# An eight-expert feed-forward layer with its tokens sorted by expert

## The reference, cut to what matters

```python
gate_scores = softmax(x @ Wg + bg)                      # 2048 tokens, 8 experts
top1_mask   = one_hot(argmax(gate_scores), 8)           # one expert a token
top1_weight = sum(gate_scores * top1_mask)
h = silu(einsum('btd,edh->bteh', x, W1) + b1)           # 256 -> 1024, each expert
o = einsum('bteh,ehd->bted', h, W2) + b2                # 1024 -> 256
x = layernorm(x + sum(o * top1_mask) * top1_weight)
```

## Time and profile before

| what | value |
|---|---|
| device time, median of 3 runs (lowest, highest) | 6390.07 us (6388.35, 6396.14) |
| device time of the profiled execution | 6391.87 us |
| its span from first to last instruction | 6390.1 us |
| mean granted TensorE clock over the span (1 is 2.4 GHz) | 0.816 |
| `L0_ffn`: first transfer of the stage, first one behind it | 2192.07 us, 3164.54 us |

### The profile page before, as it was taken

The page is one execution under the profiler, slowest core; times in us unless marked ns, Lnnn a source line. Parts: engine busy times, 40 slices in busy tenths (PEclk is TensorE's granted clock), DMA queues, the critical chain, the costliest instruction groups (busy, mean ns, idle before and its releaser), DMA issues. The chain is left out here.

```text
span 6390.1 us, 128995 instructions
## 1 busy us (share of the span) xinstructions
PE 4716.8 (74%) x51675; PEld 3223.8 (50%) x51683; DVE 3581.3 (56%) x9434; ACT 1403.9 (22%) x2503; POOL 1043.7 (16%) x1087
## 2 busy tenths in 40 slices
PE   2766767667677499999887774576685577787797
PEld 1555555555555356666555552343463345565454
DVE  7889898898894300000255455588244445444445
ACT  1222222222222121121122223111133322231111
POOL 1223232232232200000122220000010012221000
PEclk7888888888889699999988886555686687888899
DMA  1110111111100100000000000000000000000000
GB/s 49 29 28 21 29 29 26 28 25 29 29 20 22 42 14 13 26 13 13 8 0 0 31 7 12 3 0 0 36 0 5 5 4 0 26 3 6 10 17 25
DMA packets 51863, 109.59 MB, mean 17 GB/s; under 512 B 5520, under 2 KB 43792, under 8 KB 49296
## 3 DMA queue, kind: packets, MB, share of 16 engines
q1 hardware_dynamic: 51344, 102.21, 5.6%
HBM read 98.78 MB, written 3.41 MB: 16 GB/s over the span
## 5 line engine op out<-in xcount | busy, mean ns | idle before, releaser
L1603 PE MATMUL psum<-arena 128*128 128x512 f32 x1600 | 706.6, 595 | 58.4 <-DVE Y L1667 35.8
L1684 DVE SCALAR_TENSOR_TENSOR Y<-psum,arena,Y 128x256 f32<-128x256 f32 x416 | 172.5, 477 | 847.9 <-PE psum L1615 847.9
L1615 PE MATMUL psum<-arena 128*128 128x256 f32 x2624 | 583.0, 380 | 4.1 <-DVE arena L1708 4.1
L754 POOL TENSOR_TENSOR weights<-weights,arena 128x64 f32<-128x64 f32 x512 | 395.7, 794 | 1042.4 <-DVE arena L1272 1042.3
L1615 PEld LDWEIGHTS psum<-arena 128*128 128x128 f32 x2624 | 499.3, 190 | 111.7 <-issue 43.5
L144 POOL TENSOR_TENSOR arena<-arena,eps 128x4 f32<-128x4 f32 (+2 forms) x76 | 16.3, 214 | 3214.1 <-DVE arena L139 3214.1
L1603 PEld LDWEIGHTS psum<-arena 128*128 128x128 f32 x1600 | 304.4, 191 | 409.1 <-issue 341.4
L1322 DVE TENSOR_TENSOR arena<-arena 128x120 f32<-128x120 f32 (+27 forms) x1888 | 398.1, 252 | 4.3 <-DVE arena L1315 2.7
L831 PE MATMUL psum<-arena 128*32 128x1 bf16 x639 | 114.2, 179 | 385.7 <-DVE arena L1284 301.1
L1315 DVE TENSOR_TENSOR arena<-arena 128x120 f32<-128x120 f32 (+27 forms) x1888 | 390.3, 246 | 6.4 <-DVE arena L1322 2.9
L422 PE MATMUL psum<-ident,arena 128*128 128x128 f32 x1280 | 217.5, 325 | 210.4 <-ACT arena L493 210.4
(11 more groups left out here) (419 smaller groups left out, 8347.5 us busy)
## 6 DMA issues: line engine op xcount, KB each, us to landing
weights<-L_decay_rows SPq DMA_DIRECT2D x256, 160.0 KB, 3.5
arena<-in_experts_L_ffn SPq DMA_DIRECT2D x8, 2052.0 KB, 7.5
arena<-in_ctxT SPq DMA_DIRECT2D x16, 512.0 KB, 3.2
arena<-in_experts_L_ffn SPq DMA_DIRECT2D x18, 384.0 KB, 3.0
weights<-in_w_L_ffn SPq DMA_DIRECT2D x1, 3072.0 KB, 9.9
weights<-in_w_L_attn SPq DMA_DIRECT2D x1, 2881.0 KB, 12.9
weights<-in_w_L_ffn SPq DMA_DIRECT2D x1, 2753.0 KB, 11.8
weights<-in_w_L_relu SPq DMA_DIRECT2D x1, 2436.0 KB, 9.1
```

Of the source, the lines that this page charges most:

```text
L754: a = pool.tensor_tensor(blocks, bc(w.minus_eye, 1, 2), bc(beta[:, at, 2 * b:2 * b + 2], 2, Q), ALU.mult)
L1603: mm = nc.tensor.matmul(ps[:, bank, :], W[s][name][:, c, f * P:(f + 1) * P], xT[:, g, c, :], start=(c == 0), stop=(c == C - 1))
L1615: mm = nc.tensor.matmul(out, h[:, m % 2, f, u * P:(u + 1) * P], W[s]["w2"][:, f, :], start=(f == 0), stop=(f == FC - 1))
```

## The change

`L0_ffn` gets a stage function of its own, `dispatched_experts_stage`; `L3_ffn` keeps `experts_stage`. Up to the choice of the expert the head is as before. Then:

- TensorE counts, with two matmuls over the one-hot choice, how many tokens of the same tile and expert come earlier and how many each tile has for each expert. DVE makes from this the row of each token in a list sorted by expert, in which each expert's part begins at a multiple of 128 (`position_i`), and the expert that owns each tile of the list (`owner_i`). The list has 23 tiles (`SLOTS` = 16 + 8 - 1) whatever the counts are.
- SP fills the list in device memory with zeros, POOL scatters the 16 tiles of `X` into it with 16 indirect DMAs.
- For each of 23 tiles SP reads the expert's number into a register, loads this expert's weights (2180 KB: the second bias, padded to 128 rows, now travels with them) into one of three buffers, loads the tile, and stores the result of three tiles earlier. TensorE transposes the tile, makes eight blocks of hidden units with two matmuls of 128 columns each, and the way down with nine matmuls of 256 columns (one for the bias), one tile behind.
- When all 23 results lie in device memory, POOL gathers them in the tokens' order with 16 indirect DMAs, and DVE scales, adds the residual and normalises turn by turn.

The transfer of the next stage's weights moves from the stage's beginning to a place before the last three stores.

```diff
+def dispatched_experts_stage(k):
+    stage = "L0_ffn"
+    nc, ps, w, A = k.nc, k.psum, k.begin(stage), k.arena
+    E, FC = 8, 1024 // P
+    SLOTS = B + E - 1
+    BUFS = 3
+    MAGIC = 1.5 * 2 ** 23
+    sem = Semaphores(nc, stage)
+    xT_all = A(TURNS, C, N)
...
+    x_sorted = nc.dram_tensor("L0_ffn_x_sorted", (SLOTS * P, D), F32).ap()
+    y_sorted = nc.dram_tensor("L0_ffn_y_sorted", (SLOTS * P, D), F32).ap()
...
+        @block.sync
+        def _(sp):
+            sp.wait_ge(consts_set, 1)
+            sp.dma_start(x_sorted.rearrange("(s p) d -> p s d", p=P), bc(zeros, 1, SLOTS)).then_inc(zeroed, 16)
+            sp.wait_ge(placed, 2)
+            def load_weights(s):
+                if s >= BUFS:
+                    sp.wait_ge(down_ready, s - BUFS + 1)
+                e = sp.value_load(owner_i[0:1, s:s + 1], min_val=0, max_val=E - 1)
+                sp.dma_start(ew[:, s % BUFS, :], streamed[bass.ds(e, 1), :, :].rearrange("a p n -> p (a n)")
+                             ).then_inc(w_arrived[s % BUFS], 16)
+            def load_x(s):
+                if s >= BUFS:
+                    sp.wait_ge(x_turned, s - BUFS + 1)
+                sp.dma_start(xs[:, s % BUFS, :], x_sorted[s * P:(s + 1) * P, :]).then_inc(x_arrived[s % BUFS], 16)
+            def store_y(s):
+                sp.wait_ge(y_ready, s + 1)
+                sp.dma_start(y_sorted[s * P:(s + 1) * P, :], y[:, s % BUFS, :]).then_inc(y_stored[s % BUFS], 16)
+            for s in range(BUFS):
+                load_weights(s)
+            sp.wait_ge(scattered, 16 * B)
+            for s in range(BUFS):
+                load_x(s)
+            for s in range(BUFS, SLOTS):
+                load_x(s)
+                load_weights(s)
+                store_y(s - BUFS)
+            k.prefetch(sp, stage)
+            for s in range(SLOTS - BUFS, SLOTS):
+                store_y(s)
+        @block.gpsimd
+        def _(pool):
+            k.wait_weights(pool, stage)
+            pool.memset(zeros, 0.0)
+            pool.memset(ones, 1.0).then_inc(consts_set, 1)
+            turned.stage(pool, 0)
+            for g in range(TURNS - 1):
+                turned.stage_next(pool, g)
+            pool.wait_ge(placed, 1)
+            pool.wait_ge(zeroed, 16)
+            for b in range(B):
+                pool.indirect_dma_start(x_sorted, bass.IndirectOffsetOnAxis(ap=position_i[:, b:b + 1], axis=0),
+                                        k.X[:, b, :], None).then_inc(scattered, 16)
+            for i in range(BUFS):
+                pool.wait_ge(y_stored[i], 16 * len(range(i, SLOTS, BUFS)))
+            for b in range(B):
+                pool.indirect_dma_start(gathered_y[:, b, :], None, y_sorted,
+                                        bass.IndirectOffsetOnAxis(ap=position_i[:, b:b + 1], axis=0)
+                                        ).then_inc(gathered[b // TILES], 16)
+            for g in range(TURNS):
+                norm.roots(pool, g)
+        @block.tensor
...
+            pe.wait_ge(chosen, 1)
+            flat = onehot.rearrange("p b e -> p (b e)")
+            nc.tensor.matmul(ps[:, 1, 0:B * E], w.earlier, flat, start=True, stop=True)
+            nc.tensor.matmul(ps[:, 1, B * E:2 * B * E], ones, flat, start=True, stop=True).then_inc(counted, 1)
+            pe.wait_ge(placed, 1)
+            def turn_tile(s):
+                pe.wait_ge(x_arrived[s % BUFS], 16 * nth(s))
+                if s:
+                    pe.wait_ge(x_ready, s)
+                for c in range(C):
+                    mm = nc.tensor.transpose(ps[:, T_BANK, c * P:(c + 1) * P], xs[:, s % BUFS, c * P:(c + 1) * P],
+                                             k.ident)
+                mm.then_inc(x_turned, 1)
+            def up(s):
+                pe.wait_ge(w_arrived[s % BUFS], 16 * nth(s))
+                pe.wait_ge(x_ready, s + 1)
+                for f in range(FC):
+                    n = s * FC + f
+                    if n >= 4:
+                        pe.wait_ge(h_ready, n - 3)
+                    for c in range(C):
+                        mm = nc.tensor.matmul(ps[:, UP_BANK + f % 4, 0:P], W[s % BUFS]["w1"][:, c, f * P:(f + 1) * P],
+                                              xT[:, s % 2, c, :], start=(c == 0), stop=(c == C - 1))
+                    mm.then_inc(up_ready, 1)
+            def down(s):
+                pe.wait_ge(h_ready, (s + 1) * FC)
+                if s >= 2:
+                    pe.wait_ge(y_ready, s - 1)
+                out = ps[:, Y_BANK + s % 2, 0:D]
+                nc.tensor.matmul(out, ones[0:1, :], W[s % BUFS]["b2"][0:1, :], start=True, stop=False)
+                for f in range(FC):
+                    mm = nc.tensor.matmul(out, h[:, s % 2, f, :], W[s % BUFS]["w2"][:, f, :], start=False,
+                                          stop=(f == FC - 1))
+                mm.then_inc(down_ready, 1)
+            turn_tile(0)
+            for s in range(SLOTS):
+                up(s)
+                if s + 1 < SLOTS:
+                    turn_tile(s + 1)
+                if s:
+                    down(s - 1)
+            down(SLOTS - 1)
+        @block.scalar
...
+            for s in range(SLOTS):
+                for f in range(FC):
+                    act.wait_ge(up_ready, s * FC + f + 1)
+                    if f == 0 and s >= 2:
+                        act.wait_ge(down_ready, s - 1)
+                    nc.scalar.activation(h[:, s % 2, f, :], ps[:, UP_BANK + f % 4, 0:P], ACT.Silu,
+                                         bias=W[s % BUFS]["b1"][:, f:f + 1]).then_inc(h_ready, 1)
+        @block.vector
...
+            dve.wait_ge(counted, 1)
+            counts = ps[:, 1, B * E:2 * B * E].rearrange("p (b e) -> p e b", e=E)
+            chain(dve.tensor_copy(totals, counts))
...
+            dve.tensor_copy(position_i, position).then_inc(placed, 1)
+            chain(dve.tensor_tensor(past, bc(ends[:, 0:E - 1], 1, SLOTS), bc(w.slots, 2, E - 1), ALU.is_le))
+            chain(dve.tensor_reduce(owner, past, AX.X, ALU.add))
+            dve.tensor_copy(owner_i, owner).then_inc(placed, 1)
...
+            def take_x(s):
+                dve.wait_ge(x_turned, s + 1)
+                if s >= 2:
+                    dve.wait_ge(up_ready, (s - 1) * FC)
+                dve.tensor_copy(xT[:, s % 2, :, :], ps[:, T_BANK, 0:D].rearrange("p (c t) -> p c t", t=P)
+                                ).then_inc(x_ready, 1)
+            def take_y(s):
+                dve.wait_ge(down_ready, s + 1)
+                if s >= BUFS:
+                    dve.wait_ge(y_stored[s % BUFS], 16 * (nth(s) - 1))
+                dve.tensor_copy(y[:, s % BUFS, :], ps[:, Y_BANK + s % 2, 0:D]).then_inc(y_ready, 1)
+            take_x(0)
+            for s in range(SLOTS):
+                if s + 1 < SLOTS:
+                    take_x(s + 1)
+                if s:
+                    take_y(s - 1)
+            take_y(SLOTS - 1)
+            for g in range(TURNS):
+                dve.wait_ge(gathered[g], 16 * TILES)
+                for u in range(TILES):
+                    b = g * TILES + u
+                    norm.add(dve, chain, g, u, gathered_y[:, b, :], factor=weight[:, b:b + 1])
+                norm.moments(dve, chain, g)
+                norm.apply(dve, chain, g)
+    sem.release()
...
 PACKS["L0_ffn"] = lambda i: dict(wg=by_rows(i["L0_ffn_Wg"]), bg=row(i["L0_ffn_bg"]), before=before_matrix(8),
-                                 b2=np.concatenate([np.asarray(i["L0_ffn_b2"]), np.zeros((P - 8, D), np.float32)]))
+                                 earlier=np.triu(np.ones((P, P), np.float32), 1), slots=row(np.arange(B + 7, dtype=np.float32)))
...
+    b2 = np.zeros((E, P, D), np.float32)
+    b2[:, 0, :] = np.asarray(i["L0_ffn_b2"])
...
-        b1.reshape(E, -1, P).transpose(0, 2, 1)))}
+        b1.reshape(E, -1, P).transpose(0, 2, 1), b2))}
...
-    "L0_ffn": lambda k: experts_stage(k, "L0_ffn"),
+    "L0_ffn": lambda k: dispatched_experts_stage(k),
```

82 lines of the change are left out of this document (added).

## The result

The changed kernel takes 5753.51 us (median of 4 runs, 5751.02 to 5756.15), beside 6393.1 us for the kernel before in the same session: ratio 0.900, 95% interval 0.8984 to 0.9015. The forecast was 5751. The profiled execution has a span of 5751.2 us, 638.9 less than before; the sum said 638.8.

The account below looks back on a forecast made before the run. `L0_ffn` was taken as bound by TensorE, 890 us of matmuls. The new stage's terms summed to an end at 2524.7 instead of 3163.5, 638.8 us less, giving 5751 us; range 5707 to 5885.

Parts of the forecast that it names:

- the sum: All terms of the `L0_ffn` stage added in order: its end moves from 3163.5 to 2524.7, 638.8 us less.
- counts and positions: Head, after the choice: four count records at half clock, 1.2 us, and thirteen DVE steps with semaphore, 3.9 us.
- scatter, 16 indirect DMAs: Before the tiles, on POOL: 16 indirect DMAs at 1.5 us each, all on the path, 24 us.
- its landing: Between scatter and first tile load: 2.0 us, with the first three weight loads hiding behind the scatter.
- first tile: Start of the tiles: cold first way up 7.7 us, second 4.1, first way down 3.9, transposes 0.5.
- 21 tiles: Tile loop: twenty-one more tiles at a pace of 8.65 us, 181.7 us.
- gather: After the last store, on POOL: 16 indirect DMAs at 1.5 us each, all on the path, 24 us.
- the formula: Tile loop, three buffers: pace is (9.0 from free buffer to weights + 8.3 tile work) / 2 = 8.65 us.
- The indirect DMA: Scatter and gather on POOL: taken as 1.5 us each, between 0.34 and 3.1, farther 11.9; all 32 on the path.
- Dear indirect DMAs: Rival, scatter and gather: 3.1 to 21 us each, every microsecond more costing 32; up to 6400 us; chance 0.15.
- Slower than before: Rival, scatter and gather: POOL needs 21.5 us or more per indirect DMA, so the gain is gone; chance 0.02.
- The half clock: Rival, tile loop: TensorE falls back to half clock, 16.3 us a tile, 161 us go back, 5912 us; chance 0.08.

Follow-up runs that it names:

- e2: Changed kernel with four weight buffers instead of three, plus one more tile and result buffer; 5747.4 us, ratio 0.8985 to the kernel before.
- e9: Changed kernel with SP's register load moved in front of its wait for the free buffer; 5753.4 us, ratio 0.8997 to the kernel before.
- e5: Changed kernel with the first three weight loads issued behind the scatter, each after its tile load; 5760.6 us, ratio 0.9007 to the kernel before.
- e3: Changed kernel with each tile's expert a constant, s mod 8, and no register load; 5753.0 us, ratio 0.8992 to the kernel before.
- e6: Changed kernel with POOL computing the inverse roots of turns 0 to 2 between the gathers; 5751.4 us, ratio 0.8995 to the kernel before.
- e1: Changed kernel with two weight, tile and result buffers instead of three; 5979.3 us, ratio 0.9351 to the kernel before.
- e7: Changed kernel with four weight buffers and the inverse roots between the gathers together; 5743.5 us, ratio 0.8978 to the kernel before.
- e4: Changed kernel with the 16 gathers done twice, first into SBUF nobody reads; 5784.5 us, ratio 0.9042 to the kernel before.

## Why the prediction was right

The sum's terms beside what the trace shows, in order of time (the tiles' term runs from the end of the first way down to that of the last but one):

| term | forecast | measured | from |
|---|---|---|---|
| stage start to choice | 44.7 | 44.6 | 2194.98 to 2239.59 |
| counts and positions | 5.1 | 5.3 | to 2244.89 |
| scatter, 16 indirect DMAs | 24 | 20.3 | to 2265.17 |
| its landing | 2.0 | 4.7 | to 2269.84 |
| tile load, transpose, copy | 3.3 | 3.6 | to 2273.45 |
| first tile | 16.2 | 14.4 | to 2287.84 |
| 21 tiles | 181.7 | 185.3 | to 2473.09 |
| last way down | 3.9 | 4.3 | to 2477.37 |
| copy and store | 2.5 | 3.0 | to 2480.32 |
| gather | 24 | 19.8 | to 2500.14 |
| roots and norm of the first turn | 3.3 | 3.2 | to 2503.29 |
| three more turns | 21.9 | 22.7 | to 2525.97 |
| sum | 332.6 | 331.0 | |

- **The bound moved as said.** The 890 us of matmuls became 204 us for 23 tiles. The paces read from whole runs held: a tile is 8.06 us of TensorE, forecast 8.3.
- **The weights are late**, at first in every second tile, in all in 12 of 20, and the formula, half of load path plus tile, holds: e2 takes the lateness away and the pace falls to the tile's work; e9 shortens the path by 0.55 us and half of it comes back. The inputs were a little off. Register load and issue took 0.69 us where 0.5 was taken. The median landing of 8.2 is under the forecast's 7.8 and 0.7 for the neighbours, but the loads that TensorE waited for took 8.64 on average from issue to the first matmul (8.04 to 9.60): a path of 9.3 and not 9.0. A tile is 8.06 when it follows without a wait; behind a wait it is 8.33 from its first matmul to the end of its way down (2296.61 to 2304.94 in the tile shown above), since it then no longer overlaps the way down in front of it. (8.33 + 0.69 + 8.64) / 2 = 8.83; measured 8.81.
- **The indirect DMA, the widest unknown,** is 1.26 us and not 1.5: 8 us less for 32. The choice near POOL's copy was good; the sixteen transfers of the earlier trace rows would have been far off.
- **A term was mis-sized:** the scatter's landing. The weight loads were said to hide behind the scatter; they do, but they delay it, by 2.7 us more than forecast here and 8 with a fourth load (e5, e2). The delay is shown; that it is the weights' bytes on the transfer engines is estimated. The first tile was mis-sized too: the whole first way up was put at half clock, 7.7 us, and took 5.30. (Four records for the counts come to 1.0 us by the forecast's own 0.24, not 1.2.) The later landing and the slower pace cancel the cheaper indirect DMAs and first tile, so the sum is better than its terms: a hit to 1.6 us in the stage is luck where single terms are off by up to 4.
- **The rivals.** Dear indirect DMAs: no, by the rows above. Slower than before: it would have needed 21.5 us each. The half clock: it did not come in the changed kernel, but the margin was smaller than the forecast had it. The forecast counted on waits of 0.7 us; they were 1.1 on average and 1.7 at most, with clock 1.00, and with the same three buffers single waits of 1.90 to 2.37 us in e3, e5 and e6 already brought the granted clock of the next way up to about 0.7, between its two levels of 1.2 and 2.4 GHz. The Trainium skill ("TensorE: Matmul & The Clock Gate", section "HAM oscillation") describes the mechanism for a kernel whose thin tiles wait for their next slice. e1, with waits of some 8.9 us and clock 0.76, agrees; the changed kernel, with waits up to 1.7 us and clock 1.00, is not touched by it.
- **The other page's price.** "DMA: Bandwidth & Descriptors", section "Anatomy of one DMA", of the Trainium skill gives each GpSimd DMA a fixed cost of about 2 us. As a spacing it is too much: they follow one another every 1.26 us. As a latency it fits the last scatter of e5, where no weights were in flight: SP went on 1.5 us after POOL was done with it, 2.5 us after its start.

## What to carry to other kernels

When work is cut to a fraction by sorting, the stage is no longer its matmuls: here more than a third of it is routing, scatter, gather and norm, and these are worth ordering with care (28 us of 332 came back by that and one more buffer). A load that is issued one tile ahead was late by the difference between its path and a tile's work; the pace was then the mean of the two, and one more buffer brought it back to the tile's work. It also took away the waits, which near 2 us now and then cost TensorE its clock. Transfers put early "because the time is free" can slow what lands beside them, as they did the scatter here: issue as many as are needed first, and the rest behind the transfer that the path waits for.

## What the runs showed of the hardware

- An indirect DMA of 128 rows of 1 KB takes POOL 0.94 to 0.97 us in 29 of the changed kernel's 32, with 0.30 between two, scatter and gather alike; the first of the scatter takes 1.31.
- A register load from SBUF on SP, with its checks and the address, puts 0.69 us between a wait that ends and the transfer's issue. The load itself is 0.27 of it, the next operation 0.15:

```profile
L1792 SPq TENSOR_LOAD <-arena x23: 263/268/473, 2245.4 to 2455.2; - x23
L1792 SPq FUSED_REGOPS  x23: 152/152/173, 2245.9 to 2455.5; - x23
```

- The scatter's landing behind POOL's last instruction grew from 1.5 us with none or two weight loads issued before it, to 4.7 with three (4.6 to 5.1 in six runs) and 9.8 with four (e2, e7).
- After waits of 8.6 to 9.2 us the next 32 records of 128 columns took 5.17 to 6.79 us in place of 3.84 (e1). After five waits of 1.90 to 2.37 us they took 5.35 to 5.47, with granted clock 0.68 to 0.70 (e3, e5, e6); after four others of 1.83 to 2.04 us (e4, e6, e9), and after every wait of the changed kernel, at most 1.72 us, 3.84.
